# Storing gathered rows in quarters behind the additions, and loading turned one-hots ahead of them, in two pair score passes of a graph network

## The reference

```python
xl = (x @ Wl + bl).reshape(n_nodes, H, C)          # H = 5 heads, C = 64
xr = (x @ Wr + br).reshape(n_nodes, H, C)
e = jax.nn.leaky_relu(xl[src] + xr[dst], NEG_SLOPE)
alpha = jnp.einsum('ehc,hc->eh', e, att)           # the pair scores
m = jax.ops.segment_max(alpha, dst, num_segments=n_nodes)
a = jnp.exp(alpha - m[dst])
...
out = jax.ops.segment_sum(a[:, :, None] * xl[src], dst, num_segments=n_nodes)
```

## Time and profile before

| | us |
|---|---|
| median of 3 runs | 9958.47 |
| lowest and highest of them | 9952.34, 9962.12 |
| the profiled execution's own time | 9942.75 |
| its span, first to last instruction | 9940.9 |
| first pair score pass, from POOL's first issue to DVE's last score | 3498 to 4740 |
| second pair score pass | 5479 to about 6730 |

### The profile page before, as it was taken

One profiled execution on the slowest core, in us unless ns is written; L12 is line 12 of the kernel. 1 busy time (PEld: TensorE's weight loads), 2 busy tenths in 40 slices (PEclk: granted clock), 3 DMA queues, 4 the chain that ended last, 5 costly groups with the idle time before them and its releaser, 6 DMA issues. The chain is left out here.

```text
span 9940.9 us, 162652 instructions
## 1 busy us (share of the span) xinstructions
PE 7218.3 (73%) x38309; PEld 5091.7 (51%) x38310; DVE 7246.3 (73%) x10360; ACT 2340.0 (24%) x8740; POOL 5696.2 (57%) x5631
## 2 busy tenths in 40 slices
PE   6998998888888656565386566554867875878758
PEld 5776776666666533333375333333754443844437
DVE  8776444777677677777898777778987666876668
ACT  2333555000000111111496111114950000000000
POOL 5776776777677377777000777770007775067750
PEclk9998998999899777777555777775557666976669
DMA  3444554555555377777396777773964443444434
GB/s 102 114 110 111 148 147 116 152 147 147 128 147 147 84 242 248 248 248 243 136 410 265 249 250 248 248 240 143 416 263 107 96 99 68 124 113 98 97 71 120
DMA packets 843231, 1710.71 MB, mean 172 GB/s; under 512 B 385562, under 2 KB 469367, under 8 KB 787609
## 3 DMA queue, kind: packets, MB, share of 16 engines
q1 hardware_dynamic: 456542, 1132.39, 33.0%
q0 software_dynamic: 206896, 411.57, 18.5%
q10 hardware_dynamic: 179712, 165.79, 5.1%
HBM read 1264.25 MB, written 444.85 MB: 172 GB/s over the span
## 5 line engine op out<-in xcount | busy, mean ns | idle before, releaser
L532 POOL DMA_INDIRECT gathered_rows<-node_table,index x2496 | 2375.3, 952 | 928.8 <-issue 750.2
L697 PE MATMUL ps_G<-table_parts,low_onehots 125*128 125x320 bf16 x15600 | 2703.4, 340 | 130.8 <-issue 58.6
L532 POOL DMA_INDIRECT gathered_rows<-xl_table,index x1664 | 1926.9, 1158 | 1415.0 <-PEq L1505 908.7
L552 PE MATMUL ps_sum<-messages,onehots 128*125 128x65 f32 (+3 forms) x13312 | 1968.9, 313 | 494.4 <-DVE messages L1914 185.7
L532 POOL DMA_INDIRECT gathered_rows<-rel_table,index x1456 | 1384.2, 951 | 1555.0 <-ACT index L522 1111.7
L552 PEld LDWEIGHTS ps_sum<-messages,onehots 128*125 128x125 f32 x13312 | 1868.8, 226 | 635.6 <-issue 630.2
L1517 PE MATMUL ps_Z<-xr,onehots_wide 125*128 x3328 | 1475.9, 612 | 981.4 <-DVE z L1565 960.5
L697 PEld LDWEIGHTS ps_G<-table_parts,low_onehots 125*128 125x128 bf16 x15600 | 1676.0, 110 | 992.5 <-issue 74.5
L1517 PEld LDWEIGHTS ps_Z<-xr,onehots_wide 125*128 125x128 f32 x3328 | 841.9, 265 | 1615.3 <-issue 1513.5
L1565 DVE TENSOR_TENSOR z<-gathered_rows,ps_Z 128x650 f32<-128x650 f32 x832 | 653.1, 827 | 647.7 <-DMA gathered_rows<-xl_table,index 647.7
L727 DVE TENSOR_TENSOR rows_by_feature<-ps_G,fifth_onehots 128x320 f32<-128x320 f32 x1040 | 505.6, 486 | 576.8 <-PE ps_G L697 565.7
(11 more groups left out here) (329 smaller groups left out, 6742.9 us busy)
## 6 DMA issues: line engine op xcount, KB each, us to landing
stash_a<-gathered_rows SPq DMA_DIRECT2D x208, 1300.0 KB
kept_rows<-stash_a SPq DMA_DIRECT2D x208, 1300.0 KB, 7.5
onehots<-onehots_kept SPq DMA_DIRECT2D x520, 500.0 KB
onehots_turned<-onehots_turned SPq DMA_DIRECT2D x416, 256.0 KB, 5.3
stash_r<-gathered_rows ACTq DMA_DIRECT2D x208, 272.0 KB
kept_rows<-stash_r SPq DMA_DIRECT2D x208, 272.0 KB, 2.7
low_rows<-low_rows SPq DMA_DIRECT2D x416, 128.0 KB
onehots_kept<-onehots ACTq DMA_DIRECT2D x104, 500.0 KB
```

The costliest lines, as they stand in the source:

```text
L532: pool.indirect_dma_start(G[:, HALF * k + q, 0:width], None, table, bass.IndirectOffsetOnAxis(IDX[:, k, q:q + 1], 0)).then_inc(gathered[k] ...
L552: return nc.tensor.matmul(ps_sum[0:BN, bass.ds(at, width)], S[:, j, :], M, start=False, stop=True, skip_group_check=True)
L697: last = nc.tensor.matmul(ps_G[:, (fetch * k + g) % 2, 0:D * FIVE], OT[0:BN, k, g, a, :], HP[:, part, a, :, :].rearrange("p f b -> p (f b) ...
```

## The change

Two things in SP's list of `pair_scores`, and what follows from them in the counters.

First, the stash of a group is no longer one DMA of 8 chunks (1300 KB) that waits for the gathers. It is four DMAs of two chunks (325 KB each), and each waits for the addition over its two chunks (`z_made`), which in turn was made after the gathers landed. Second, the load of turned one-hots stands in front of the group's stashes, not behind. Each slot's semaphore `stashed[k]` now rises by 64 in a turn (four DMAs of 16), and POOL waits for that. POOL's, PE's, ACT's and DVE's lists hold the same instructions as before.

```diff
+            PAIRS = HALF // 2
...
                             for k in range(K):
-                                stash_group(sp, G, GW, stash_a, i, k)
-                                if last_turn and k >= K // 2:
-                                    continue
-
-                                ahead, slot = i + (k + K // 2) // K, (k + K // 2) % K
-                                sp.wait_ge(z_made.sem, z_made.at(4 * (K * i + k - 1)))
-                                sp.sem_inc(sp_seen, 1)
-                                load_turned(sp, ST, ahead, slot)
+                                if not (last_turn and k >= K // 2):
+                                    ahead, slot = i + (k + K // 2) // K, (k + K // 2) % K
+                                    sp.wait_ge(z_made.sem, z_made.at(4 * (K * i + k - 1)))
+                                    sp.sem_inc(sp_seen, 1)
+                                    load_turned(sp, ST, ahead, slot)
+                                for e in range(PAIRS):
+                                    j = HALF * k + 2 * e
+                                    sp.wait_ge(z_made.sem, z_made.at(4 * (K * i + k) + e + 1))
+                                    sp.sem_inc(sp_seen, 1)
+                                    sp.dma_start(stash_a[bass.ds(K * i + k, 1), :, 2 * e * GW:2 * (e + 1) * GW].rearrange("o p r -> (o p) r"),
+                                                 G[:, j:j + 2, :].rearrange("p c f -> p (c f)")).then_inc(stashed[k].sem, 16)
...
-                            pool.wait_ge(stashed[k].sem, stashed[k].at(16 * i))
+                            pool.wait_ge(stashed[k].sem, stashed[k].at(16 * PAIRS * i))
```

More of the change, by code:

```diff
@@ L1490, in _ @@
                         for k in range(K):
-                            sp.wait_ge(stashed[k].sem, stashed[k].at(16 * TURNS))
+                            sp.wait_ge(stashed[k].sem, stashed[k].at(16 * PAIRS * TURNS))
                     @block.gpsimd
@@ L1601, in _ @@
                         turn(TURNS - 1, True)
-                for c in (*loaded, *stashed):
+                for c in loaded:
                     c.over(16 * TURNS)
+                for c in stashed:
+                    c.over(16 * PAIRS * TURNS)
                 for c in gathered:
```

## The result

| | us |
|---|---|
| before, median of 4 runs | 9958.97 (9952.34 to 9962.12) |
| after, median of 4 runs | 9851.23 (9846.46 to 9858.84) |
| ratio, 95% interval | 0.9893 [0.9876, 0.9911] |
| profiled execution, before | 9942.75, span 9940.9 |
| profiled execution, after | 9846.46, span 9843.9 |

From POOL's first issue of a pass to DVE's last score the first pass shrank from 1241.9 to 1191.1 us and the second from 1240.7 to 1184.6: 106.9 us together, the whole difference.

The account below looks back on a forecast made before the run. The prediction took POOL's issue time plus holds by DVE's two-input L1572 as the bound. 208 x 0 + 2 us on the profiled 9942.75 gave 9944.8; with the median 15.7 us higher it forecast 9960, no change, range 9860 to 10002.

Parts of the forecast that it names:

- What bounds the kernel: Mid-pass: POOL's issue time, 10.0 us per eight gathers, plus 1.72 us of holds by DVE's two-input L1572.
- The frame: POOL's fifth issue is held by L1572 while L is under 2.42; each 0.1 us of L costs 21 us.
- L: Time from the end of a group's eighth POOL issue to DVE's first add of that group; about 2.2 us before.
- Stash later and in quarters costs nothing on POOL's side: POOL needs the stash only a turn later; some 35 us of slack, so no cost on the path.
- SP's queue: Four waits and issues for one: five steps at 0.69 us take 3.5 of 11.76 us a group.
- The load ahead hides a wait that nobody feels: The turned one-hots leave 5.8 us sooner and shrink ACT's 3 us wait; gain nothing, as DVE waits for gathers.
- I take L unchanged: DMA engines: late transfers, stacked up, end by 13.2 us against 13.5 allowed for the eighth gather; cost 0 us.
- Rival B: Eighth gather so late that the fifth issue escapes L1572: faster, 9825 to 9910, about 9850; chance 0.12.
- Rival A: Eighth gather late by 0.1 to 0.2 us, fifth issue still held: slower, 9980 to 10002, about 9990; chance 0.12.
- C: Rival: the eighth gather lands sooner, L down by 0.1 to 0.2 us: faster, 9920 to 9940; chance 0.07.
- D: Rival: SP's transfers pay a fixed cost serially, 13.0 us a group: slower, +270 us, 10230; chance 0.05.
- Start and end of a pass: One more load before the first gathers, 0.8 us, and 1 us either way at the end; +2 us for two passes.

Follow-up runs that it names:

- one_input_weigh: Kernel before, with the two-input L1572 replaced by an equally long reduction with one SBUF input, leaving part of the computation out; 9597.0 us, ratio 0.9648.
- idle_sum_04: Kernel before, plus a useless 320-element sum on DVE ahead of each group's first add, no transfer touched; 9829.0 us, ratio 0.9881.
- half_stash_late: Changed kernel, but the third and fourth stash quarters wait only for the second addition, so stash and load leave early; 9944.4 us, ratio 0.9997.
- quarters_at_once: Kernel before, with the stash in four quarters sent together when the gathers have landed, the load behind them; 9945.7 us, ratio 0.9998.
- load_in_front: Kernel before, one whole stash at the old moment, but the load of turned one-hots in front of it; 9945.0 us, ratio 0.9999.
- quarters_load_behind: Changed kernel with its late quarters, but the load of turned one-hots behind the group's last quarter; 9933.2 us, ratio 0.9987.
- switch_halfway: Changed kernel, but quarters leave at once up to turn 12 and late from turn 13 in the first pass, reversed in the second; 9889.6 us, ratio 0.9947.
- idle_sum_01: Kernel before, plus a useless 32-element sum on DVE ahead of each group's first add, no transfer touched; 9930.2 us, ratio 0.9989.
- whole_stash_late: Changed kernel, but the stash goes as one 1300 KB transfer behind the last of the group's four additions; 9800.5 us, ratio 0.9858.
- load_between: Changed kernel, but the load of turned one-hots stands between the second and third stash quarters; 9869.8 us, ratio 0.9921.
- weigh_in_four: Kernel before, with L1572 split into four instructions of 320 elements, computation complete; 9636.1 us, ratio 0.9688.
- after_weigh_in_four: Changed kernel, with L1572 split into four instructions of 320 elements; 9655.2 us, ratio 0.9706.

## Why the prediction was wrong

- **What bounds the kernel: right.** The period is POOL's issue time plus the holds by L1572: 10.0 us a group with the holds taken out (one_input_weigh), 11.76 with them.
- **The frame: right.** L decides, and the lock ends near 2.42: idle_sum_04 crossed it at 2.57 and gained, half_stash_late stayed at 2.22 and did not.
- **Stash later and in quarters costs nothing on POOL's side: right.** POOL's waits for the stash between 3520 and 4660 us sum to 1.5 us. Four for one is free (quarters_at_once).
- **SP's queue: right.** Quarters and load left when forecast (E + 9.03 for 9.0).
- **The load ahead hides a wait that nobody feels: right alone, wrong in company.** load_in_front gained nothing; with late quarters the load behind them cost 0.9%, some 93 us, against the changed kernel (quarters_load_behind, 0.9987 against 0.9893).
- **"I take L unchanged": this step failed**, in its term for the DMA engines. The sum let two late quarters push the load by at most 0.6 us beyond its 2.6, to E + 12.2, and had the engines free by 13.2. In switch_halfway, with the old rhythm still intact, the load was through at E + 13.6, and the eighth gather's add came at E + 15.04, not 14.0. In the changed kernel the median load needs 4.8 us. With 4.8 in the place of 3.2 the same stack ends at 9.0 + 4.8 + 1.0 = 14.8, beyond the 13.5 that were allowed. The unit of 1.0 us a quarter came from one landing in the earlier trace rows, early in the period, as the difference of two landings; it did not hold later, where the engines spent 1.5 us at 94 GB/s on packets of the gathers. The margin that it left, 0.3 us, was smaller than its error.
- **A second fault: the sum was made once, for the old rhythm.** SP's transfers follow DVE's adds, so a late add makes the next group's transfers later against its eighth gather: L went 2.18, 3.30, 4.73 in three groups. The question was not how far L moves but whether 2.2 stays a place where it can rest.
- **Rival B: right in mechanism, in size partly by luck, too small in chance.** Its price was 11.1 to 11.5 us a group, measured 11.2; its time about 9850, measured 9851.2. It was worked out at L = 2.5 to 2.9, though, where the truth is 4.6, another tooth of the saw; that the periods there are alike (11.1 to 11.5, and 11.03 at 4.6) is luck. The group without a long issue that it forecast is not to be found in the changed kernel: all 192 mid-pass groups have two, of 1.09 us or more. It appears in idle_sum_04, at an L that B took. Other signs came: the long issues changed place. The range left out the lower half of B and so missed by 9 us.
- **Rivals A, C, D** did not happen. Rival A's band, L between 2.3 and 2.42, is 0.1 us wide; idle_sum_01 aimed at it, and 14 of 96 groups fell over the edge. So little room hardly deserved the same chance as B.
- **Start and end of a pass: right, within its size.** 103 x 0.50 = 51.5 us less in the first pass against 50.8 measured.

**Open.** Why transfers in the second half of a period take so long is not settled. The bytes of a group are the same in all these kernels. From 3800 to 4400 us the packets of the gathers take 39.0% of the DMA engines' time for 67.9 MB before, 39.2% for 67.9 in half_stash_late, 40.9% for 67.9 in quarters_at_once and 39.0% for 72.3 in whole_stash_late, but 46.3% for 70.6 in the changed kernel and 45.2% for 70.4 in load_between. So the share of 0.83 comes largely from gather packets that take longer; it goes with late quarters, neither with quarters alone nor with a late stash in one piece. What holds up these packets no run shows, and since L is long in whole_stash_late too, they are not the whole cause of a long L.

## What to carry to other kernels

Where GpSimd issues indirect DMAs back to back, look at the longest of them and at which VectorE instruction was running: if it has two SBUF inputs, try splitting it into short ones before anything else is tuned (here 3.1%). Two loops of fixed beat that disturb each other have a sawtooth, not a slope: a wait that grows may well speed them up, a forecast has to ask on which tooth the kernel comes to rest, and gains by a shift of phase (1.1% here) are gone once the hold itself is removed. When a budget of transfers ends within a few tenths of a microsecond of its limit, give the other side half of the chance, above all if the transfers are released by the work that they delay.

## What the runs showed of the hardware

- **Useless work made the kernel faster**: 0.49 us more for VectorE in each of 208 groups took 1.2% off, 1.8 us took 2.5% off.
- **The hold is for the instruction, not for the work**: in the kernel before one of 1.48 us held issues for up to 1.24 us (2.19 for 0.95), four in a row with the same elements, 1.68 us, mostly let an issue through in 1.28 or less (weigh_in_four), though some missed every gap and took up to 1.80 (after_weigh_in_four). A held issue ended 0.82 after L1572.
- **A load's landing depends much on its surroundings**: 256 KB took 2.6 us at the start of a pass, 4.5 to 4.8 in load_between, half_stash_late and the changed kernel, 5.7 behind four quarters at once, 5.9 right behind a full stash.
- **Two rhythms in one execution**: in switch_halfway the passes kept an L of about 4.6 with late quarters and 2.2 with early ones, and went from one to the other within three groups.
